# Moving the maxima of the first attention to ScalarE's DMA queue, its bias into the rows of keys, its weights three batches behind, and taking one root for a norm of a norm

## The reference, cut to what matters

```python
x = x + tanh(g_xattn[0]) * L0_xattn(ctx, layernorm(x), b, itok)    # 16 heads of 8, the context's keys, bias over keys
x = x + tanh(g_ffn[0]) * L0_ffn(layernorm(x), ...)
x = x + tanh(g_xattn[1]) * L1_xattn(layernorm(x), ctx, ...)        # 16 heads of 8, the context's keys and x's own, no bias
x = x + tanh(g_ffn[1]) * L1_ffn(layernorm(x), ...)                 # 16 heads of 4, causal; then 8 experts
x = x + tanh(g_xattn[2]) * L2_xattn(ctx, layernorm(x), mask, b)    # 8 heads of 16, bias over keys
x = x + tanh(g_ffn[2]) * L2_ffn(layernorm(x), ...)                 # 8 experts
x = x + tanh(g_xattn[3]) * L3_xattn(layernorm(x), ctx, lens, ...)  # starts with rmsnorm(layernorm(x)), no softmax
x = x + tanh(g_ffn[3]) * L3_ffn(layernorm(x), ...)                 # quantised gate, up and down
```

## Time and profile before

| | us |
|---|---|
| median of 3 runs | 2066.76 |
| the profiled execution's own time | 2063.91 |
| its span, first to last instruction | 2062.1 |
| PE busy | 1650.3 (80%) |
| DVE busy | 1209.1 (59%) |
| ACT busy | 1042.4 (51%) |
| POOL busy | 686.4 (33%) |

### The profile page before, as it was taken

How to read it: one execution, slowest core, us unless ns; L and a number is a source line. 1 busy time by engine, 2 the same in 40 slices (tenths; PEclk the granted TensorE clock), 3 DMA queues, 4 the chain that set the end, 5 groups by cost and what they waited for, 6 DMA issues and landing times. The chain is left out here.

```text
span 2062.1 us, 42577 instructions
## 1 busy us (share of the span) xinstructions
PE 1650.3 (80%) x14902; PEld 1071.9 (52%) x14902; DVE 1209.1 (59%) x3694; ACT 1042.4 (51%) x2171; POOL 686.4 (33%) x1196
## 2 busy tenths in 40 slices
PE   1788997999998999868998996667577688788544
PEld 0333444677665666544444665555344477676332
DVE  3454555544436889845887655454665542366666
ACT  1344443433325777644554563534344565486556
POOL 4343310120003333212555312731667430541460
PEclk9995558999997999978999998888755698898756
DMA  7544426630005555331222211353745122321100
GB/s 198 127 92 110 120 58 184 205 82 1 0 1 125 127 133 142 73 111 44 68 64 62 75 49 63 91 143 96 191 100 129 57 67 71 107 87 39 45 26 21
DMA packets 191504, 184.65 MB, mean 90 GB/s; under 512 B 26528, under 2 KB 174944, under 8 KB 189984
## 3 DMA queue, kind: packets, MB, share of 16 engines
q1 hardware_dynamic: 182288, 145.22, 27.1%
q10 hardware_dynamic: 816, 19.92, 3.2%
q0 software_dynamic: 8192, 16.79, 2.9%
HBM read 119.67 MB, written 80.74 MB: 97 GB/s over the span
## 5 line engine op out<-in xcount | busy, mean ns | idle before, releaser
L2209 DVE TENSOR_REDUCE mneg<-psb 128x4 f32<-128x512 f32 (+1 forms) x576 | 383.3, 684 | 206.2 <-PE psb L1803 198.7
L2583 ACT ACTIVATE HB<-psb 128x512 f32<-128x512 f32 x384 | 218.7, 596 | 147.5 <-PE psb L1803 143.5
L1803 PE MATMUL psb<-K,Q 48*128 48x128 bf16 (+1 forms) x1280 | 192.5, 265 | 114.0 <-DMA Q<-sc_q 44.5
L1803 PE MATMUL psb<-Q,K 51*128 51x128 bf16 (+2 forms) x1664 | 267.2, 301 | 5.5 <-ACT HB L2583 2.3
L2802 POOL TENSOR_SCALAR rs<-mv 128x2 f32<-128x2 f32 (+1 forms) x96 | 21.9, 229 | 654.7 <-DVE mv L2169 652.4
L1803 PEld LDWEIGHTS psb<-K,Q 48*128 48x128 bf16 (+1 forms) x1280 | 111.8, 113 | 204.7 <-issue 134.6
L2583 ACT ACTIVATE HB<-psb,bias 128x512 f32<-128x512 f32 x192 | 131.2, 685 | 169.5 <-PE psb L1803 168.6
L1803 PEld LDWEIGHTS psb<-Q,K 51*128 51x128 bf16 (+2 forms) x1664 | 177.1, 138 | 29.7 <-issue 11.6
L1803 PE MATMUL psb<-HB,VA 128*9 128x128 f32 (+1 forms) x2560 | 164.0, 340 | 5.2 <-ACT OE L2588 4.7
L1803 PE MATMUL psb<-KS,Q 48*128 48x128 bf16 x1024 | 140.0, 228 | 25.6 <-DMA Q<-mT 11.3
L1803 PE MATMUL psb<-biasT,selbb 96*128 96x512 bf16 x192 | 109.9, 572 | 0.0
(11 more groups left out here) (480 smaller groups left out, 3816.6 us busy)
## 6 DMA issues: line engine op xcount, KB each, us to landing
K<-sc_k SPq DMA_DIRECT2D x96, 192.0 KB, 3.7
Q<-sc_q SPq DMA_DIRECT2D x96, 192.0 KB
tok_rows<-in_zero ACTq DMA_DIRECT2D x16, 1152.0 KB, 32.8
sc_q<-comp SPq DMA_DIRECT2D x48, 192.0 KB, 2.2
K<-tok_rows SPq DMA_DIRECT2D x72, 128.0 KB, 2.1
sc_q<-comp SPq DMA_DIRECT2D x48, 128.0 KB, 2.1
vraw<-in_ctx SPq DMA_DIRECT2D x48, 128.0 KB, 4.7
KS<-sc_s SPq DMA_DIRECT2D x32, 192.0 KB
```

What stands on the lines that cost most here:

```text
L1803: return pe.e.matmul(out, w, x, start=start, stop=stop, skip_group_check=True)
L2209: t = e.tensor_reduce(m.mneg[:, s.b % 4, s.i * A.per:(s.i + 1) * A.per], PSB[s.use.bank].rearrange("p (h k) -> p h k", h=A.per), AX.X, ALU ...
L2583: a.done(act(m.HB[:, s.slot, :], PSB[s.use.bank], ACT.Exp, bias=bz), s.use.drained)
```

## The change

- The first attention's maxima (`BY_ACT`) are moved by two DMAs that ACT issues right behind its copy to `mT`, in place of SP.
- Its lag is 3 in place of 2.
- Its bias is no longer a matmul and no longer ACT's operand. The turned bias, three parts of it, is copied to DRAM as 3 rows under the 48 rows of keys (6 DMAs in the new step `bias_store`), K8's load brings 51 rows, and the queries have ones in the 3 rows. All attentions with heads of 8 or 4 get 51 rows, and the maxima lie at rows 51 to 53.
- In the second attention, which has no bias, the queries' 3 rows must be zero: 3 DMAs at the start write zeros to the scratch, and its Q8 loads bring 51 rows (K8's bring 48, KS's 48).
- The setup fills Q8's places with ones as well as K8's.
- The norm of a norm is `(var (1 + eps) + eps^2) ^ -0.5`: four operations on POOL and one power.
- `reckon` has new costs for these steps.

```diff
@@ reckon
-        "norm_in": lambda: (("dve", 450 * s.n), ("pool", {None: 2000 if s.rms else 1600, "second": 3200, "both": 4100}[s.twice])),
+        "norm_in": lambda: (("dve", 450 * s.n), ("pool", {None: 2000 if s.rms else 1600, "second": 3200, "both": 1900}[s.twice])),
-        "max_rows": lambda: (("pe", 130), ("act", 290), ("sp", 650 * A.halves)),
+        "max_rows": lambda: (("pe", 130), ("act", 1500)) if A.name in BY_ACT else (("pe", 130), ("act", 290), ("sp", 650 * A.halves)),
@@ class Attention
-        self.n_rows, self.halves = (96, 1) if dh == 16 else (48, 2)
+        self.n_rows, self.halves = (96, 1) if dh == 16 else (51, 2)
+        self.bias_rows = bias_i is not None and dh != 16
-        self.lag = 2 if H == 16 else 4
+        self.lag = 4 if H == 8 else 3 if name in ('a0',) else 2
@@ make_plan
     do("setup", cst=t_cst, ints=t_i, g=t_g, cols=t_cols, uses=biasu)
+    do("bias_store", need=t_biasT)
+    t_bias_rows = dma("dma_bias", 6)
+    t_zero_rows = dma("dma_zeros", 3)
@@ tensor_program
-        if A.bias_i is not None:
+        if A.bias_i is not None and not A.bias_rows:
             t = matmul(o4, m.selbb[:, s.b:s.b + 1].broadcast_to([96, 128]), m.biasT[:, A.bias_i, :].unsqueeze(1).broadcast_to([96, 4, 128]),
                        False, True, False)
@@ scalar_program
         a.done(act(m.mT[0:n, s.k, :], PSB[s.use.bank].bitcast(BF16)[0:n, 0:128], ACT.Copy), s.use.drained)
+        if s.A.name in BY_ACT:
+            a.wait_ge(s.use.drained, s.rows)
+            for half in range(s.A.halves):
+                a.e.dma_start(max_place(m, s, half), m.mT[24 * half:24 * half + 24, s.k, :]).then_inc(a.sems[f"dma_m{s.k}"], 16)
-        if A.bias_i is not None:
+        if A.bias_i is not None and not A.bias_rows:
             a.wait_ge(s.bias)
             bz = m.bias[:, A.bias_i, s.b:s.b + 1]
@@ pool_program, norm_in
+        if s.twice == "both":
+            then(e.tensor_scalar(r0, var, 1.0 + EPS, EPS * EPS, ALU.mult, ALU.add))
+        if s.twice != "second":
@@ sync_program, rows_load
+            rows = sc[p].rearrange("c (d h) t -> (c d) h t", d=A.dh)
+            if s.sc == "sc_q1" or s.sc == "sc_k" and A.bias_rows:
+                rows = m.longer[s.sc][p].rearrange("(r h) t -> r h t", h=16)
+            n = rows.shape[0]
             for half in range(2):
-                src = sc[p].rearrange("c (d h) t -> (c d) h t", d=A.dh)[:, 8 * half:8 * half + 8, :]
-                load(name, dst[64 * half:64 * half + 6 * A.dh, :].rearrange("r (h t) -> r h t", h=8), src)
+                load(name, dst[64 * half:64 * half + n, :].rearrange("r (h t) -> r h t", h=8), rows[:, 8 * half:8 * half + 8, :])
+    def bias_store(s):
+        sp.wait_ge(s.need)
+        rows = m.longer["sc_k"][:, 768:816, :].rearrange("p (c h) t -> p c h t", c=3)
+        zero = m.longer["sc_q1"][:, 768:816, :].rearrange("p (c h) t -> p c (h t)", c=3)
+        for c in range(3):
+            for b in range(2):
+                src = m.biasT[32 * c + b:32 * c + 32:2, 0, :].unsqueeze(1).broadcast_to([16, 16, 128])
+                load("bias", rows[:, c, :, 128 * b:128 * b + 128], src)
+        for c in range(3):
+            load("zeros", zero[:, c].bitcast(F32), io["zero"][0:16, :])
```

More of the change, by code:

```diff
@@ L111, in reckon @@
         "v_copy": lambda: (("dve", 330),),
-        "scores": lambda: (("pe", (230 if not s.beside else 130) + (220 if A.bias_i is not None or A.causal else 0)), ("dve", 720)),
+        "scores": lambda: (("pe", (230 if not s.beside else 130) + (220 if A.bias_i is not None and not A.bias_rows or A.causal else 0)), ("dve", 720)),
         "max_parts": lambda: (("dve", 1050),),
-        "max_rows": lambda: (("pe", 130), ("act", 290), ("sp", 650 * A.halves)),
+        "max_rows": lambda: (("pe", 130), ("act", 1500)) if A.name in BY_ACT else (("pe", 130), ("act", 290), ("sp", 650 * A.halves)),
         "weights": lambda: (("pe", (230 if not s.scores else 130) + (220 if A.causal else 0)), ("act", 640 if A.bias_i is None else 720)),
@@ L422, in scratch @@
             return nc.dram_tensor(name, [NP, 6, n, 256], BF16, kind="Internal").ap()
-        self.scratch = {n: scratch(n) for n in ("sc_k", "sc_q0", "sc_q1", "sc_q3", "sc_s")}
+        self.scratch = {n: scratch(n) for n in ("sc_q0", "sc_q3", "sc_s")}
+        self.longer = {n: nc.dram_tensor(n, [NP, 51 * 16, 256], BF16, kind="Internal").ap() for n in ("sc_k", "sc_q1")}
+        self.scratch |= {n: a[:, 0:768, :].rearrange("p (c q) t -> p c q t", c=6) for n, a in self.longer.items()}
         self.scratch |= {n: scratch(n, 64) for n in ("sc_f0", "sc_f1")}
@@ L905, in loaded @@
             prepare(p, coming.pop(p)[-1]())
-        load_step = {p: max(2 * (p - A.R) + 1 + lag, 2 * p - 4) for p in range(NP)}
+        load_step = {p: max(2 * (p - A.R) + 1 + lag + (1 if A.own and lag == 3 else 0), 2 * p - 4) for p in range(NP)}
         ahead = [p for p in range(NP) if load_step[p] < 0]
@@ L1786, in heads, with max_place @@
     return m.place(tile, A.at(p))[64 * half:64 * half + A.n_rows + rows_, o:o + 128]
+def max_place(m, s, half):
+    o = 128 * (s.b % 2)
+    return m.place(m.Q8, s.A.at(s.b // 2))[s.A.max_rows(half), :].rearrange("c (h t) -> c h t", h=8)[:, :, o:o + 128]
 def v_heads(vt, p, b2, A):
@@ L1853, in scores @@
     def scores(s):
-        s["last"] = s.A.bias_i is None and not s.A.causal
+        s["last"] = (s.A.bias_i is None or s.A.bias_rows) and not s.A.causal
         if s.beside:
@@ L2751, in setup @@
     def setup(s):
-        ones(m.K8, 2, count())
-        ones(m.K8, 3, count())
+        for at in (2, 3):
+            ones(m.Q8, at, count())
+            ones(m.K8, at, count())
         g.wait_ge(before[0])
@@ L2800, in norm_in @@
             then(e.tensor_scalar(r0, r0, EPS, None, ALU.add))
-        else:
+        elif s.twice != "both":
             then(e.tensor_scalar(r0, var, EPS, None, ALU.add))
-        if not s.twice:
+        if s.twice == "both":
+            then(e.tensor_scalar(r0, var, 1.0 + EPS, EPS * EPS, ALU.mult, ALU.add))
+        if s.twice != "second":
             if s.by == "act" and not s.rms:
@@ L2814, in norm_in @@
         then(e.tensor_scalar(r0, r0, EPS, None, ALU.add))
-        if s.twice == "second" and s.by == "act":
+        if s.by == "act":
             then(e.tensor_tensor(r0, r0, power, ALU.pow))
             shift()
-        elif s.twice == "second":
+        else:
             done(e.tensor_tensor(r0, r0, power, ALU.pow), s.rstd)
-        else:
-            then(e.tensor_tensor(r0, r0, power, ALU.pow))
-            if s.by == "act":
-                then(e.tensor_tensor(r1, r1, r0, ALU.mult))
-                shift()
-            else:
-                done(e.tensor_tensor(r1, r1, r0, ALU.mult), s.rstd)
     def split(s):
@@ L2913, in max_rows @@
     def max_rows(s):
-        A = s.A
-        o = 128 * (s.b % 2)
+        if s.A.name in BY_ACT:
+            return
         sp.wait_ge(s.use.drained, s.rows)
-        for half in range(A.halves):
-            dst = m.place(m.Q8, A.at(s.b // 2))[A.max_rows(half), :].rearrange("c (h t) -> c h t", h=8)[:, :, o:o + 128]
-            if True:
-                load(f"m{s.k}", dst, m.mT[24 * half:24 * half + 24, s.k, :])
-            else:
-                for c in range(3):
-                    load(f"m{s.k}", dst[c:c + 1], m.mT[24 * half + 8 * c:24 * half + 8 * c + 8, s.k, :])
+        for half in range(s.A.halves):
+            load(f"m{s.k}", max_place(m, s, half), m.mT[24 * half:24 * half + 24, s.k, :])
     def moe1_load(s):
```

15 lines of the change are left out of this document (9 added, 6 removed).

## The result

The kernel after the change took 2077.99 us (median of 16 runs, 2071.92 to 2089.23) where the kernel before took 2067.49 (16 runs, 2031.26 to 2077.46) beside it. The ratio is 1.019 with a 95% interval of 1.015 to 1.023; it leaves out runs more than 1.5% above the fastest of their kernel, which for the kernel before, whose fastest run is 2031, drops most of its runs. The medians over all runs have a ratio of 1.005, and a second measurement of the same pair (e5) came out at 1.0045 (1.0005 to 1.0085). So the change makes the kernel slower, by about 0.5% over all runs and by up to 2% against the fastest runs of the kernel before, where 2035 us, 1.5% faster, was forecast.

What follows compares the result with a forecast made beforehand. PE was taken to set the first attention's pace, DVE and PE both near their limit in the second. 2063.9 - 52 + 24 - 4 = 2031.9, plus 2.9 for the median, gives 2035 us; range 2000 to 2082.

Steps and rivals of the forecast that it cites:

- slower: Rival: second attention's maxima wait behind Q's loads in SP's queue, K's loads cost too; 2089 us, chance 0.15.
- I take a third of the 5.0 us: Second attention: Q's 51-row loads hold SP's queue 1.7 us longer a pair, 24 us against the change, between 0 and 70.
- the upper bound: Q's 51-row load in the second attention costs as much as one of ten times the bytes: 8.7 us, not 3.7.
- I take 0, up to 1 us a pair: First attention: K's 51-row loads cost nothing, since needed some three batches after issue and no longer before maxima.
- The sum for the first attention: First attention: PE 185, ACT 161, DVE 154 us of work give a stage of 226 us, bounds 208 to 247.
- PE's 185 us: First attention: PE's busy time falls from 249.7 us by 65 us without the bias matmul.
- The rival with a larger gain: Rival: without the bias matmul the first attention's clock could rise to 2.4 GHz; 2006 us, chance 0.20.
- I take 3 us against the change: First attention: a lag of 3 loses overlap for one batch, 3 us against the change, between 0 and 4.8.
- So the two long stalls go: First attention: with ACT issuing the maxima, not behind SP's stores and loads, stalls of 10.0 and 9.1 us vanish.
- no gain where it is meant: Rival: ACT's 1.4 us holds make PE run dry 1 us a batch in the first attention; 2065 us, chance 0.15.
- The start: Before the first attention: 15 weight loads behind SP's 9 DMAs delay the first store by 3 us, between 0 and 4.3.
- The norm of a norm: Near the end: four norms on POOL, each 2.25 us shorter, save 4 us, between 2.25 and 9.0.

Runs made afterwards that it cites:

- e5: The kernel after, unchanged, measured a second time beside the kernel before: ratio 1.0045, first attention 243.3 us, second 291.0 us.
- e1: The kernel after with each of Q's 51-row loads in the second attention split into 48 and 3 rows: ratio 0.984 to the kernel before.
- e6: The kernel after with each of Q's 51-row loads in the second attention split into 49 and 2 rows: ratio 0.989 to the kernel before.
- e2: The kernel after with each of K's 51-row loads in the first attention split into 48 and 3 rows: ratio 0.993 to the kernel before.
- e3: The kernel after with both Q's and K's 51-row loads split into 48 and 3 rows: ratio 0.969 to the kernel before.
- e4: e3 with the first attention's maxima issued by SP again, lag of 3 kept: ratio 0.968 to the kernel before.
- e8: The kernel after with K's loads split 48 + 3, Q's of 48 rows only, zero rows written once, weights loaded later: ratio 0.971 to the kernel before.
- e9: e3 measured once more, on the chip of other runs: ratio 0.975 to the kernel before, first attention 214.7 us.
- e14: e8 with v's load first in each pair (first and third attention) and a lag of 3 in the second attention too: ratio 0.966 to the kernel before.
- e7: The kernel before with ACT instead of SP issuing the first attention's maxima: ratio 1.005, first attention 288.3 us.
- e16: The kernel before with a lag of 3 in the first attention, same program as e12, measured again: ratio 0.989, first attention 242.5 us.
- e12: The kernel before with a lag of 3 instead of 2 in the first attention: ratio 0.982, first attention 218.7 us.

## Why the prediction was wrong, point by point

**The direction.** The right mechanism stood there as the rival "slower": maxima behind Q's loads in SP's queue. I gave it 0.15 and "I take a third of the 5.0 us", 24 us in all, "near the lower row", because 51 rows are only 6% more bytes than 48. Measured are 48.7 us in the stage, 3.5 us for each of 14 pairs; this is the term that failed, by its size and not by its mechanism. The bytes were the wrong argument: e1 has the same bytes and a stage of 241.0 us where the kernel before has 236.9 and 240.3, and e6 has about 0.30 of the loss. The rule of the Trainium skill (page "DMA: Bandwidth & Descriptors", section "Why a DMA increments its semaphore by 16 and not by 1") spoke for the upper bound; 3.5 us a pair is nearer to its 5.0 than to my 1.7, and the order of e1, e6 and the kernel after agrees with the rule.

**"I take 0, up to 1 us a pair" for K's loads.** Wrong, by the same form: 240.4 against 213.9 to 219.2 us once they are split, 21 to 26 us or 1.3 to 1.7 a pair. I had asked who needs K, and not who needs what stands behind K in the queue: v's load landed 4.1 us later, DVE stood before its copy with the maxima of the next batch behind it, and PE stood behind DVE.

**The sum for the first attention.** 226 + 3 us were forecast and 240.4 came; without K's form it is 214 to 222 (e2, e3, e4, e8, e9), within the bounds of 208 to 247 and 7 to 15 us better than forecast. PE's 185 us came out as 173.6 and the exponential at its 598 ns. So the size of the stage was right but for K. The rival with a larger gain had PE's clock rise to 2.4 GHz; from 140 us to the end of the stage it was 0.65 where it was 0.57. The reasons for the size were not right:

**"I take 3 us against the change", for the lag of 3.** This was the step that carries the gain. Of four kernels with SP's maxima, lag 2 gives 282.7 and 287.7 us with the bias matmul and 265.7 with bias rows, lag 3 gives 218.7 to 242.5 and 220.5. A lag is the time that the maxima have from DVE's last maximum to PE's use. I had seen that PE goes on 4 us after SP begins the row of maxima and had looked for the cure in the queue. What bias rows add to the lag is that PE is no longer full, so that the stage hardly depends on the clock: 210.2 to 221.9 us in the seven profiles that have both and K's load split, against 218.7, 242.5 and 245.9 in three with the bias matmul. PE's busy time in two of the seven is 158.7 and 172.5 us (e3 and e14), and the stages are 213.9 and 213.7.

**"So the two long stalls go", with the maxima on ACT.** They go (e7), and it is worth nothing by itself, and 6 us at the lag of 3 (e4 against e3), about what one execution differs from the next. An issue on ACT takes 0.73 us, not 0.66, as the row of those in the kernel after has it (min/median/max ns):

```profile
L2596 ACTq DMA_DIRECT2D Q<-mT x64: 728/729/1406, 62.5 to 280.9; - x64
```

Two of them take 1.5 us, but the exponentials have only 12.6 us under "issue" in the whole stage, and PE waits 2.4 us for them. So the rival "no gain where it is meant" is not what happened.

**The start.** The first store was issued at 33.16 against 30.16, the 3 us forecast. The first scores came 8.5 us later, since K's first load lands later too: with K split alone they came at 48.5 (e2), 3.3 us later than before.

**The norm of a norm.** 2.04 us from one to the next (2015.83 - 2013.79), and the last stretch is 5.9 us shorter where I took 4, within 2.25 to 9. But this holds only at the lower level of time (126.5 us in four profiles with the change, 132.4 and 132.7 without). At the other level the stretch takes 136.8 to 138.4 us in nine profiles with the short norm and 137.0 to 137.6 in four without it: there the same edit gains nothing, and why is open. So the 4 us of the forecast hold for one of the two levels only.

**What stays open.** Causal attention and experts were 10.5 us longer in the profile, but this stretch took 559.4 to 574.4 us in six profiles at the lower level (559.4 and 566.6 without the change, 560.2, 569.9, 569.9 and 574.4 with it), so I read no effect from it. The stretch before the last `y_rows<-Q` was 7.8 us shorter there (307 to 311 with the change in four profiles, 315 and 318 without), and not at the other level (335 to 340 either way); no run was made for it. That the clock is higher with the lag of 3 because PE pauses less is a reading of the traces, not shown by a run. The part of the lag's gain that comes from the later loads and not from the slack of the maxima was not taken apart.

## What to carry to other kernels

Don't price a load by its bytes: when its number of rows stops being a multiple of 16, split off the odd rows (48 + 3 for 51). Price a slower load on everything behind it in its queue, and follow who stands in strict order behind that. And where PE stands still for a small result that makes a round trip over other engines, try the distance in the pipeline first: it is one number, and here it was worth more than another queue for the result, and more than the removal of a quarter of PE's work (37 to 69 us, against 0 to 6 for the queue and 17 to 22 for the bias rows at the old lag).

## What the runs showed of the hardware that I had not expected

- The two wide loads of Q are issued in 0.65 us, and two of K's 48-row loads in 0.92, so the issue shows nothing of the cost; it is in the transfers behind: v's 128 KB landed after 8.8 and 9.6 us instead of 4.7 and 5.2, and from the first issue of the 6 KB of maxima to PE's step 7.0 and 7.8 us passed instead of 4.1 and 3.6.
- Loads of 51, 49 + 2 and 48 + 3 rows gave a second attention of 285.6, 254.6 and 241.0 us and landings of v after 9.6, 6.3 and (48 rows alone) 5.2 us: a load is not either even or odd, its cost has steps between.
- PE can be full for 65 us at 0.50 and, with the same kinds of instructions, be granted 0.84 in the next 25 (e16), and for 110 us at 0.50 in the kernel before (195 to 305 us); one program's stage was 218.7 us in one execution and 242.5 in another. The bias matmul alone does not hold the clock at 0.50: e12 has 1.00 from 175 to 263 us with it.
